# A fused attention and FFN layer on one core: the FFN's bias leaves TensorE and is added by the output transfers

## The chip, the cores and the metric

The kernel runs on one core of one Trainium2 chip. The metric is the device time of one execution in microseconds (us). Before the change it is 4342.03 us, the median of three runs (4333.88 to 4343.93).

## The reference, cut to what matters

```python
# x is (4, 2048, 512) float32, 16 heads of 32; the layer norms have no learned scale
x = x + attention(layernorm(x))          # softmax attention with a band bias, then Wo and bo
x = x + ffn(layernorm(x))                # x of this line is called x1 in the kernel

def ffn(x):                              # one linear layer
    xd = mx_quantize_and_scale_back(x)   # blocks of 32, scale = max|x| / 7.5, FP6 grid
    wd = mx_quantize_and_scale_back(weight)
    return xd @ wd.T + bias              # bias: 512 values, added to each of the 8192 rows
```

The output is therefore x1 + xd @ wd.T + bias for each of 8192 rows of 512 values, 16 MB in all.

## The kernel before, in words

The program has three stages, each a block of its own in which all engines start together.

`project` normalises x and makes q, k and v, which it leaves in device memory. `attend` runs over 64 units (16 groups of four heads in a batch, four chunks of 512 queries each), each unit over 16 steps `kt` of 128 keys. `finish` takes the 8192 rows in 16 chunks of 512 rows, and a chunk as four tiles of 128 rows.

**Attention.** TensorE makes the maxima of a unit ahead of its scores (L624), the scores (L643), the weighted sums (L657) and the sums of the softmax (L666). ScalarE makes the exponentials (L715), VectorE the maxima (L725) and the band (L752). GpSimd adds pairs of steps (L790) and issues five transfers a unit that add one pair buffer onto another in on-chip memory (L795, 1 MB each, `merged` counts them). The sync engine (SP) issues all other transfers in an order written out by hand: in each unit the stores of the unit before (L544, L548), the loads of q, k and v for the next group (L525, L530, L534), and at `kt` 14 the transfer L539, which puts the next unit's maxima into the row `shift` of its q tile. TensorE's first score of the next unit waits for it.

**The last stage.** For chunk c SP loads `o_raw` (L850), four transfers `o_rec` that spread each row of reciprocals over 32 partitions (L854) and `xb` (L859). GpSimd multiplies `o_raw` by `o_rec` (L901), ScalarE makes the high part (L930), GpSimd the low part (L905). TensorE projects (`out_project`, L1043), VectorE adds `xb` (x1, L980), takes the statistics, and after ScalarE's normalisation quantises (L952 to L965, the last gives `xd`). TensorE turns `xd` (`turn`, L1052), ScalarE and VectorE split it into `t_hi` and `t_lo` (L915, L972), TensorE multiplies by the FFN's weights (`linear`, L1070), and VectorE's `last_sum` (L996) adds x1 into `res`, one of two buffers, which SP stores (`store`, L863).

TensorE's order in iteration c is: `out_project(c + 1)` tiles 0 and 1, `turn(c)`, `out_project(c + 1)` tiles 2 and 3, `linear(c)`. Each tile of `out_project` or `linear` is 12 products of 128 x 128 by 128 x 512. In `linear` each tile begins with one more product, of a 2 x 128 tile of ones with `fb`, the bias in two parts (L1062). It starts the accumulation, so it puts the bias into the result. `fb` is prepared at the start of the stage by a load (L869), ScalarE (L935), VectorE (L1010) and a small transfer (L876).

SP's order in iteration c of this stage is `load_xb(c + 2)`, `load_o(c + 4)`, `store(c)`. `load_o(c)` waits until the low parts of chunk c - 2 are made. GpSimd's order is, for each chunk, four L901 and four L905. `last_sum` of chunk c waits until the store of chunk c - 2 has landed.

Of the kernel before, what the change touches and what calls it, by code (L numbers as in the profile page):

```python
# [14 lines left out]
P = 128  # L15
# [33 lines left out]
def f32(ap):  # L49

    return ap.bitcast(F32)


def build(nc, x, wq, wk, wv, wo, bq, bk, bv, bo, ocr_bias, ffn_w, ffn_b, out):
    x_ch = x.rearrange("(c t p) d -> c p t d", t=TT, p=P)
    out_ch = out.rearrange("(c t p) d -> c p t d", t=TT, p=P)

    def dram(name, shape):
        return nc.dram_tensor(name, shape, F32, kind="Internal").ap()


    q_hi_d, q_lo_d = dram("q_hi_d", (NHG * NCH, P, CH)), dram("q_lo_d", (NHG * NCH, P, CH))
    k_hi_d, k_lo_d = dram("k_hi_d", (NHG * NCH, P, CH)), dram("k_lo_d", (NHG * NCH, P, CH))
    v_d = dram("v_d", (NHG * NCH, TT, P, P))
    xb_d = dram("xb_d", (NCH, P, TT, D))
    wo_hi_d, wo_lo_d = dram("wo_hi_d", (P, KB, D)), dram("wo_lo_d", (P, KB, D))
    wd_hi_d, wd_lo_d = dram("wd_hi_d", (P, KB, D)), dram("wd_lo_d", (P, KB, D))
    o_d = dram("o_d", (NHG * NCH, P, CH))
    sum_d = dram("sum_d", (NHG * NCH, HG, CH))
    rec_d = dram("rec_d", (NHG * NCH, HG, CH))  # L70

    ctx = ExitStack()
    with ctx:
        def sem(name):
            return ctx.enter_context(nc.semaphore(name))

        ident = ctx.enter_context(nc.sbuf_tensor("ident", [P, P], F32))
        band_f = ctx.enter_context(nc.sbuf_tensor("band_f", [P, P + 2 * BAND_R], F32))
        project(nc, sem, ident, band_f, x_ch, wq, wk, wv, wo, bq, bk, bv, bo, ocr_bias, ffn_w,
                q_hi_d, q_lo_d, k_hi_d, k_lo_d, v_d, xb_d, wo_hi_d, wo_lo_d, wd_hi_d, wd_lo_d)  # L80
        attend(nc, sem, ident, band_f, q_hi_d, q_lo_d, k_hi_d, k_lo_d, v_d, o_d, sum_d, rec_d)
        finish(nc, sem, ident, ffn_b, xb_d, wo_hi_d, wo_lo_d, wd_hi_d, wd_lo_d, o_d, sum_d, rec_d, out_ch)
# [338 lines left out]
def attend(nc, sem, ident, band_f, q_hi_d, q_lo_d, k_hi_d, k_lo_d, v_d, o_d, sum_d, rec_d):  # L421
# [31 lines left out]
        sem("pv_done"), sem("sum_done"), sem("o_copied"), sem("sum_copied"), sem("o_out"), sem("sum_out"))  # L453
    den_loaded, den_inverted, rec_out = sem("den_loaded"), sem("den_inverted"), sem("rec_out")
# [46 lines left out]
    with ctx:  # L501
# [20 lines left out]
        def _(sp):  # L522
# [42 lines left out]
            for unit in range(NU + 1):  # L565
                g, u = unit // QC, unit % QC
                for kt in range(KT):
# [11 lines left out]
                    if unit == NU:  # L579
                        continue  # L580

# [20 lines left out]
            sp.wait_ge(sum_out, 16 * NU)  # L602
            sp.wait_ge(rec_out, 16 * (NG - 1))
# [195 lines left out]
def finish(nc, sem, ident, ffn_b, xb_d, wo_hi_d, wo_lo_d, wd_hi_d, wd_lo_d, o_d, sum_d, rec_d, out_ch):  # L799
# [5 lines left out]
    wo_in, wd_in, o_in, xb_in, fb_in = (  # L805
        [sem(f"wo_in{i}") for i in range(2)], sem("wd_in"), [sem(f"o_in{i}") for i in range(2)],
        [sem(f"xb_in{i}") for i in range(2)], sem("fb_in"))
# [3 lines left out]
    fb_split, fb_ready, consts2 = sem("fb_split"), sem("fb_ready"), sem("consts2")  # L811
# [9 lines left out]
    with ctx:  # L821
# [12 lines left out]
        fb_raw, fb_low = sb("fb_raw", [1, D]), sb("fb_low", [1, D], F32R)  # L834
        fb, ones2 = sb("fb", [2, D], F32R), sb("ones2", [2, P], F32R)
# [9 lines left out]
        def _(sp):  # L845
# [15 lines left out]
            def store(c):  # L861
                sp.wait_ge(res_ready, TT * c + TT)
                sp.dma_start(out_ch[c], res[:, c % 2]).then_inc(out_done[c % 2], 16)  # L863

# [4 lines left out]
            sp.dma_start(fb_raw[:], ffn_b.unsqueeze(0)).then_inc(fb_in, 16)  # L869
# [5 lines left out]
            sp.wait_ge(fb_split, 2)  # L875
            sp.dma_start(f32(fb[1:2, :]), f32(fb_low[:])).then_inc(fb_ready, 16)  # L876
# [4 lines left out]
            for c in range(NCH):  # L881
                if c + 2 < NCH:
                    load_xb(c + 2)
                if c + 4 < NCH:
                    load_o(c + 4)
                store(c)
# [4 lines left out]
        def _(pool):  # L891
            nc.gpsimd.memset(eps2[:], EPS).then_inc(consts2, 1)
            nc.gpsimd.memset(f32(ones2[:]), 1.0).then_inc(consts2, 1)
            for c in range(1, NCH):
                b = c % 2
# [7 lines left out]
                for g in range(NHG):  # L903
                    pool.wait_ge(o_high, NHG * c + g + 1)
                    nc.gpsimd.tensor_tensor(o_lo[:, b, g, :], o_raw[:, b, g, :], f32(o_hi[:, b, g, :]),  # L905
                                            ALU.subtract).then_inc(o_split, 1)

        @block.scalar
        def _(act):
# [23 lines left out]
            act.wait_ge(consts2, 2)  # L933
            act.wait_ge(fb_in, 16)
            nc.scalar.activation(fb[0:1, :], fb_raw[:], ACT.Copy).then_inc(fb_split, 1)  # L935
# [11 lines left out]
        def _(v):  # L947
# [61 lines left out]
            v.wait_ge(fb_split, 1)  # L1009
            nc.vector.tensor_tensor(fb_low[:], fb_raw[:], f32(fb[0:1, :]), ALU.subtract).then_inc(fb_split, 1)  # L1010
# [16 lines left out]
        def _(pe):  # L1027
# [27 lines left out]
            def linear(c):  # L1055
                for t in range(TT):
# [5 lines left out]
                    nc.tensor.matmul(ps_r[:, t, :], ones2[:], fb[:], start=True, stop=False)  # L1062
                    for k in range(KB):
# [5 lines left out]
                        for j, (lhs, rhs) in enumerate(terms):  # L1069
                            last = nc.tensor.matmul(ps_r[:, t, :], lhs, rhs, start=False,  # L1070
# [4 lines left out]
            for c in range(NCH):  # L1075
# [5 lines left out]
                if c == 0:  # L1081
                    pe.wait_ge(consts2, 2)
                    pe.wait_ge(fb_ready, 16)
# [28 lines left out]
```

## Time and profile before

| | |
|---|---|
| median of three runs | 4342.03 us (4333.88 to 4343.93) |
| the profiled execution | 4340.61 us, span of its instructions 4338.8 us |
| granted TensorE clock, mean | 0.983 of full speed |
| TensorE products busy | 4207.4 us, 97% of the span |
| VectorE, GpSimd, ScalarE busy | 3304.7, 2934.3, 2407.7 us |
| attention, about | 560 to 3860 us of the span |
| last stage, about | 3863 to 4339 us of the span |

A row of a window gives its start and end, its length, the busy time of TensorE's products, TensorE's weight loads, VectorE, ScalarE and GpSimd (with counts), the granted clock, the mean busy share of the 16 DMA engines and what they moved in GB/s. A row of a timeline gives the start, the length (of x4: of the four together), the engine, the line, the operation and its operands; in brackets stands how long the engine was idle before and what ended that. A TensorE product's own length overlaps the next one's, so the distance of two starts is what one costs. SPq is the issue of a transfer by SP.

### The profile page before, as it was taken

How to read it: one execution, taken by the hardware profiler on the slowest of the kernel's cores; microseconds unless marked ns; L12 is line 12 of the kernel's file. 1: busy time of each engine (PE TensorE's matmuls, PEld its weight loads, DVE VectorE, ACT ScalarE, POOL GpSimd, SP SyncE). 2: the span in 40 equal slices, each digit the busy share in tenths (PEclk: the TensorE clock that was granted, in tenths of full speed). 3: DMA queues.
4: the chain of work that ended last, by engine and by line, in shares of the span. 5: the costliest groups of instructions: out<-in, count | busy, mean ns of one | idle time of the engine just before them, and what ended most of it. 6: DMA issues, size and time to landing. Idle time of an engine off the chain costs nothing. (4 is left out here: it accounts for less than half of the span.)

```text
span 4338.8 us, 61851 instructions
## 1 busy us (share of the span) xinstructions
PE 4207.4 (97%) x22416; PEld 2580.4 (59%) x22416; DVE 3304.7 (76%) x5623; ACT 2407.7 (55%) x4652; POOL 2934.3 (68%) x983
## 2 busy tenths in 40 slices
PE   7999989999999999999999999999999999968999
PEld 6888855555555555555555555555555555526777
DVE  6444448888888888888888888888888888717776
ACT  2222216666666666666666666666666666623222
POOL 2111116888888887888888888888888888846552
PEclk9999979999999999999999999999999999979999
DMA  7666654676676766676766767666777666565442
GB/s 258 207 208 205 210 155 107 143 165 138 140 159 144 170 136 154 136 160 145 164 135 143 158 143 169 135 154 138 161 146 162 139 142 143 114 149 183 165 159 73
DMA packets 265423, 674.19 MB, mean 155 GB/s; under 512 B 26561, under 2 KB 93121, under 8 KB 219074
## 3 DMA queue, kind: packets, MB, share of 16 engines
q0 software_dynamic: 46080, 335.56, 38.7%
q1 hardware_dynamic: 219074, 335.10, 26.0%
q8 instruction: 161, 2.64, 0.2%
q14 instruction: 108, 0.88, 0.1%
HBM read 195.04 MB, written 139.46 MB: 77 GB/s over the span
## 5 line engine op out<-in xcount | busy, mean ns | idle before, releaser
L725 DVE TENSOR_REDUCE part_max<-ps_m 128x1 f32<-128x512 f32 x4096 | 2513.4, 680 | 501.3 <-PE ps_m L624 501.1
L790 POOL TENSOR_TENSOR pair<-p_sb 128x2048 f32<-128x2048 f32 x512 | 2413.8, 4723 | 419.0 <-ACT p_sb L715 211.7
L715 ACT ACTIVATE p_sb<-ps_s 128x512 f32<-128x512 f32 x4096 | 2084.5, 617 | 762.0 <-PE ps_s L643 758.3
L643 PE MATMUL ps_s<-q_st,k_st 97*128 97x512 f32 x4096 | 1687.5, 413 | 8.8 <-DMA q_st<-shift 6.3
L624 PE MATMUL ps_m<-k_st,q_st 96*128 96x512 f32 x4096 | 1641.8, 404 | 20.3 <-POOL k_st L779 20.1
L643 PEld LDWEIGHTS ps_s<-q_st,k_st 97*128 97x128 f32 x4096 | 772.7, 189 | 663.4 <-issue 430.4
L657 PE MATMUL ps_o<-p_sb,v_sb 128*32 128x512 f32 x8192 | 994.4, 603 | 13.3 <-DVE p_sb L752 5.6
L624 PEld LDWEIGHTS ps_m<-k_st,q_st 96*128 96x128 f32 x4096 | 786.8, 192 | 189.0 <-DVE part_max L725 37.2
L657 PEld LDWEIGHTS ps_o<-p_sb,v_sb 128*32 128x32 f32 x8192 | 225.0, 109 | 495.0 <-ACT p_sb L715 315.1
L795 POOL DMA_DIRECT2D pair<-pair x320 | 280.2, 876 | 182.1 <-POOL pair L790 153.7
L172 POOL TENSOR_TENSOR xb<-xin,bo_row 128x2048 f32<-128x2048 f32 x16 | 75.1, 4693 | 423.8 <-DMA xin<-in_x 413.3
L752 DVE TENSOR_TENSOR p_sb<-p_sb,band_f 128x520 f32<-128x520 f32 (+2 forms) x352 | 192.5, 575 | 51.3 <-ACT p_sb L715 51.3
L309 DVE SCALAR_TENSOR_TENSOR s_lo<-ps_p,bias,s_hi 128x512 fp32r<-128x512 f32 x128 | 96.0, 750 | 169.8 <-ACT s_hi L354 169.8
L354 ACT ACTIVATE s_hi<-ps_p,bias 128x512 fp32r<-128x512 f32 x128 | 88.1, 688 | 241.8 <-PE ps_p L405 233.4
L905 POOL TENSOR_TENSOR o_lo<-o_raw,o_hi 128x512 fp32r<-128x512 f32 x60 | 125.8, 2127 | 134.7 <-ACT o_hi L930 134.7
L405 PE MATMUL ps_p<-x_hi,w_hi 128*128 128x512 f32 x512 | 203.2, 397 | 4.2 <-DVE x_lo L294 4.1
L405 PE MATMUL ps_p<-x_hi,w_lo 128*128 128x512 f32 x512 | 200.8, 392 | 0.0
L405 PE MATMUL ps_p<-x_lo,w_hi 128*128 128x512 f32 x512 | 199.2, 389 | 0.0
L666 PE MATMUL ps_m<-pair,ones 128*32 128x512 f32 x1536 | 178.2, 595 | 9.1 <-DMA pair<-pair 9.1
L701 ACT ACTIVATE sum_st<-ps_m 128x512 f32<-128x512 f32 x64 | 38.2, 597 | 259.7 <-PE ps_m L666 259.7
L1043 PE MATMUL ps_r<-wo_hi,o_hi 128*128 128x512 f32 x256 | 103.6, 405 | 42.3 <-DVE o_lo L1005 27.3
L319 DVE TENSOR_TENSOR v_st<-ps_p,bv_row 128x512 f32<-128x512 f32 x64 | 44.1, 691 | 119.8 <-PE ps_p L405 119.8
(97 smaller groups left out, 2632.4 us busy)
## 6 DMA issues: line engine op xcount, KB each, us to landing
pair<-pair POOLq DMA_DIRECT2D x320, 1024.0 KB, 8.3
q_st<-q_hi_d SPq DMA_DIRECT2D x128, 256.0 KB, 6.9
k_st<-k_hi_d SPq DMA_DIRECT2D x128, 256.0 KB, 5.9
xin<-in_x SPq DMA_DIRECT2D x16, 1024.0 KB, 8.3
xb_d<-xb SPq DMA_DIRECT2D x16, 1024.0 KB, 5.2
q_hi_d<-s_hi SPq DMA_DIRECT2D x64, 256.0 KB, 2.0
q_lo_d<-s_lo SPq DMA_DIRECT2D x64, 256.0 KB, 2.3
k_hi_d<-s_hi SPq DMA_DIRECT2D x64, 256.0 KB, 2.3
```

Of the source, the lines that this page charges most:

```text
L405: last = nc.tensor.matmul(ps_p[:, n % RING], lhs, rhs, start=(k == 0 and j == 0), stop=(k == KB - 1 and j == 2))
L624: nc.tensor.matmul(ps_m[:, bank, :], q_st[0:ROWS, u, h, t * P:(t + 1) * P], k_st[0:ROWS, g % 2, n, h, :], start=True, stop=True).then_inc( ...
L643: nc.tensor.matmul(ps_s[:, (HG * s + h) % RING_S, :], k_st[0:ROWS + 1, unit // QC % 2, kt // TT, h, kt % TT * P:(kt % TT + 1) * P], q_st[0 ...
L657: last = nc.tensor.matmul(ps_o[h * HD:(h + 1) * HD, :], v_sb[:, kt, h * HD:(h + 1) * HD], p_sb[:, s % SLOTS, h, :], start=(kt == 0), stop= ...
L666: last = nc.tensor.matmul(ps_m[h * HD:(h + 1) * HD, bank, :], ones[:], pair[:, (PAIRS * unit + n) % PAIR_RING, h, :], start=(n == PAIRS - ...
L715: nc.scalar.activation(p_sb[:, s % SLOTS, h, :], ps_s[:, (HG * s + h) % RING_S, :], ACT.Exp, scale=SCALE).then_inc(p_ready, 1)
L725: nc.vector.tensor_reduce(part_max[:, unit % 2, col, n:n + 1], ps_m[:, max_place(unit, j) % RING_M, :], AX.X, ALU.max).then_inc(max_taken, 1)
L752: nc.vector.tensor_tensor(view, view, factor, ALU.mult).then_inc(banded, 1)
L790: nc.gpsimd.tensor_tensor(pair[:, m % PAIR_RING], p_sb[:, s % SLOTS], p_sb[:, (s + 1) % SLOTS], ALU.add).then_inc(paired, 1)
L795: pool.dma_start(pair[:, m % PAIR_RING], pair[:, (m - CHAINS) % PAIR_RING], accum_op=ALU.add).then_inc(merged[n % CHAINS], 16)
L905: nc.gpsimd.tensor_tensor(o_lo[:, b, g, :], o_raw[:, b, g, :], f32(o_hi[:, b, g, :]), ALU.subtract).then_inc(o_split, 1)
L1043: last = nc.tensor.matmul(ps_r[:, t, :], lhs, rhs, start=(k == 0 and j == 0), stop=(k == NHG - 1 and j == 2))
```

## The change

In attention SP gets one more transfer in each of the first 16 units, at `kt` 13: it fills one chunk of the output (1 MB, 512 rows of 2 KB) with the bias, read again and again from its 2 KB in device memory. A wait for all of them stands at the end of the stage. In the last stage the bias products, `fb` and all that prepared it are gone. The store moves from SP to GpSimd and becomes a transfer that adds `res` onto what stands in the output. GpSimd issues the store of chunk c - 4 ahead of its work on chunk c, and the last four stores behind all its other work.

```diff
 # attend, SP, in unit `unit` at step kt, ahead of put_shift(unit + 1) at kt 14
+                    if unit < NCH and kt == 13:
+                        sp.dma_start(out_ch[unit], ffn_b.unsqueeze(0).unsqueeze(0).to_broadcast([P, TT, D])).then_inc(bias_out, 16)
...
             sp.wait_ge(sum_out, 16 * NU)
+            sp.wait_ge(bias_out, 16 * NCH)
 # finish, SP
-            def store(c):
-                sp.wait_ge(res_ready, TT * c + TT)
-                sp.dma_start(out_ch[c], res[:, c % 2]).then_inc(out_done[c % 2], 16)
...
-            sp.dma_start(fb_raw[:], ffn_b.unsqueeze(0)).then_inc(fb_in, 16)
...
-            sp.wait_ge(fb_split, 2)
-            sp.dma_start(f32(fb[1:2, :]), f32(fb_low[:])).then_inc(fb_ready, 16)
...
                 if c + 4 < NCH:
                     load_o(c + 4)
-                store(c)
 # finish, GpSimd
-            nc.gpsimd.memset(f32(ones2[:]), 1.0).then_inc(consts2, 1)
+            def store(c):
+                pool.wait_ge(res_ready, TT * c + TT)
+                pool.dma_start(out_ch[c], res[:, c % 2], accum_op=ALU.add).then_inc(out_done[c % 2], 16)
+
             for c in range(1, NCH):
+                if c > 3:
+                    store(c - 4)
...
+            for c in range(NCH - 4, NCH):
+                store(c)
 # finish, ScalarE and VectorE
-            act.wait_ge(fb_in, 16)
-            nc.scalar.activation(fb[0:1, :], fb_raw[:], ACT.Copy).then_inc(fb_split, 1)
...
-            v.wait_ge(fb_split, 1)
-            nc.vector.tensor_tensor(fb_low[:], fb_raw[:], f32(fb[0:1, :]), ALU.subtract).then_inc(fb_split, 1)
 # finish, TensorE, linear(c), each of four tiles
-                    nc.tensor.matmul(ps_r[:, t, :], ones2[:], fb[:], start=True, stop=False)
...
-                            last = nc.tensor.matmul(ps_r[:, t, :], lhs, rhs, start=False,
+                            last = nc.tensor.matmul(ps_r[:, t, :], lhs, rhs, start=(k == 0 and j == 0),
```

## Rows read from the trace of the kernel before

**Rows 1.** Busy time by stretch: attention, and the last stage when steady
```profile
560.00:3860.00 3300.00, 3248.43 (x18147) 1819.15 (x18146) 2701.10 (x4609) 2156.23 (x4236) 2649.14 (x834) 0.99 0.68 146
4004.00:4200.00 196.00, 196.00 (x878) 151.48 (x876) 150.08 (x237) 53.76 (x95) 106.74 (x61) 1.00 0.47 167
```
**Rows 2.** The chain that ended last, shares of the span by line
```profile
by line: PE ps_r L1070 4.1%; PE ps_r L1043 3.5%; SPq L854 0.9%; PE ps_t L1052 0.6%; PE ps_r L1062 0.6%; DMA o_rec<-rec_d 0.3%; POOL o_raw L901 0.1%; SPq L866 0.1%; issue 0.1%; DVE res L996 0.1%; SPq L872 0.1%; DVE xd L965 0.1%; DVE y_q L960
```
**Rows 3.** Timeline of TensorE's products with and without a bias product between
```profile
4081.93 0.39 PE L1070 MATMUL ps_r<-wd_hi,t_lo 128*128 128x512 f32 x1
...
4082.16 0.39 PE L1043 MATMUL ps_r<-wo_hi,o_hi 128*128 128x512 f32 x1
...
4094.59 0.39 PE L1043 MATMUL ps_r<-wo_lo,o_hi 128*128 128x512 f32 x1
...
4094.91 0.50 PE L1062 MATMUL ps_r<-fb,ones 2*128 2x512 f32 x1
...
4095.33 0.50 PE L1070 MATMUL ps_r<-wd_hi,t_hi 128*128 128x512 f32 x1
...
4095.67 0.39 PE L1070 MATMUL ps_r<-wd_lo,t_hi 128*128 128x512 f32 x1
```
**Rows 4.** Timeline: xd made and turned, chunks 1 and 2, then steady
```profile
3953.92 2.28 DVE L965 TENSOR_TENSOR xd<-y_q,qs 128x2048 f32<-128x2048 fp8e4 x1
...
3956.87 1.91 PE L1052 MATMUL ps_t<-ident,xd 128*128 128x128 f32 x16
...
3977.99 3.44 DVE L965 TENSOR_TENSOR xd<-y_q,qs 128x2048 f32<-128x2048 fp8e4 x1
...
3983.01 1.91 PE L1052 MATMUL ps_t<-ident,xd 128*128 128x128 f32 x16
...
4081.20 2.28 DVE L965 TENSOR_TENSOR xd<-y_q,qs 128x2048 f32<-128x2048 fp8e4 x1
...
4087.60 1.91 PE L1052 MATMUL ps_t<-ident,xd 128*128 128x128 f32 x16
```
**Rows 5.** The end: the last turn and linear (timeline), the last sum (chain)
```profile
4317.92 1.97 PE L1052 MATMUL ps_t<-ident,xd 128*128 128x128 f32 x16 [0.28 <-DVE xd L965]
...
4320.24 0.50 PE L1070 MATMUL ps_r<-wd_hi,t_hi 128*128 128x512 f32 x1
...
4333.41 0.69 DVE res L996
```
**Rows 6.** Timeline of GpSimd, and VectorE's last sum of a chunk
```profile
4101.56 9.22 POOL L905 TENSOR_TENSOR o_lo<-o_raw,o_hi 128x512 fp32r<-128x512 f32 x4 [11.93 <-ACT o_hi L930]
...
4109.55 0.68 DVE L996 TENSOR_TENSOR res<-ps_r,x 128x512 f32<-128x512 f32 x1
...
4110.74 5.03 POOL L901 TENSOR_TENSOR o_raw<-o_raw,o_rec 128x512 f32<-128x512 f32 x4
```
**Rows 7.** Busy time by stretch: DMA idle, one merge alone, one chunk's transfers
```profile
928.00:936.00 8.00, 7.99 (x56) 4.05 (x55) 5.94 (x10) 4.04 (x9) 5.64 (x2) 1.00 0.00 0
946.00:952.00 6.00, 6.00 (x39) 3.38 (x35) 5.31 (x11) 4.06 (x8) 5.45 (x4) 1.00 0.87 176
4085.00:4094.00 9.00, 9.00 (x50) 7.68 (x49) 6.54 (x10) 2.07 (x4) 4.63 (x4) 1.00 0.99 342
4094.00:4104.80 10.80, 10.80 (x44) 7.54 (x42) 8.23 (x18) 5.32 (x9) 3.24 (x3) 1.00 0.27 104
```
**Rows 8.** The page: GpSimd's issue of an adding transfer, and its landing
```profile
L795 POOL DMA_DIRECT2D pair<-pair x320 | 280.2, 876 | 182.1 <-POOL pair L790 153.7
...
pair<-pair POOLq DMA_DIRECT2D x320, 1024.0 KB, 8.3
```
**Rows 9.** Timeline of SP in the fourth unit: last load, then the shift
```profile
841.37 0.38 SPq L534 DMA_DIRECT2D v_sb<-v_d  x1
855.10 0.52 SPq L539 DMA_DIRECT2D q_st<-shift  x1
```
**Rows 10.** Line L539 alone: who waited for it, us and times
```profile
  PEld ps_s L643: 13.7, 16
```

More of the change, by code:

```diff
@@ L80, in build @@
                 q_hi_d, q_lo_d, k_hi_d, k_lo_d, v_d, xb_d, wo_hi_d, wo_lo_d, wd_hi_d, wd_lo_d)
-        attend(nc, sem, ident, band_f, q_hi_d, q_lo_d, k_hi_d, k_lo_d, v_d, o_d, sum_d, rec_d)
-        finish(nc, sem, ident, ffn_b, xb_d, wo_hi_d, wo_lo_d, wd_hi_d, wd_lo_d, o_d, sum_d, rec_d, out_ch)
+        attend(nc, sem, ident, band_f, q_hi_d, q_lo_d, k_hi_d, k_lo_d, v_d, o_d, sum_d, rec_d, ffn_b, out_ch)
+        finish(nc, sem, ident, xb_d, wo_hi_d, wo_lo_d, wd_hi_d, wd_lo_d, o_d, sum_d, rec_d, out_ch)
 def blocks(ap):
@@ L418, in _, with attend @@
                     products(c, n)
-def attend(nc, sem, ident, band_f, q_hi_d, q_lo_d, k_hi_d, k_lo_d, v_d, o_d, sum_d, rec_d):
+def attend(nc, sem, ident, band_f, q_hi_d, q_lo_d, k_hi_d, k_lo_d, v_d, o_d, sum_d, rec_d, ffn_b, out_ch):
     NU = NG * QC
@@ L453, in attend @@
         sem("pv_done"), sem("sum_done"), sem("o_copied"), sem("sum_copied"), sem("o_out"), sem("sum_out"))
+    bias_out = sem("bias_out")
     den_loaded, den_inverted, rec_out = sem("den_loaded"), sem("den_inverted"), sem("rec_out")
@@ L796, in _, with finish @@
                                    accum_op=ALU.add).then_inc(merged[n % CHAINS], 16)
-def finish(nc, sem, ident, ffn_b, xb_d, wo_hi_d, wo_lo_d, wd_hi_d, wd_lo_d, o_d, sum_d, rec_d, out_ch):
-    wo_in, wd_in, o_in, xb_in, fb_in = (
+def finish(nc, sem, ident, xb_d, wo_hi_d, wo_lo_d, wd_hi_d, wd_lo_d, o_d, sum_d, rec_d, out_ch):
+    wo_in, wd_in, o_in, xb_in = (
         [sem(f"wo_in{i}") for i in range(2)], sem("wd_in"), [sem(f"o_in{i}") for i in range(2)],
-        [sem(f"xb_in{i}") for i in range(2)], sem("fb_in"))
+        [sem(f"xb_in{i}") for i in range(2)])
     rec_in = [sem(f"rec_in{i}") for i in range(2)]
@@ L810, in finish @@
     den_in, den_turned, rec_last = sem("den_in"), sem("den_turned"), sem("rec_last")
-    fb_split, fb_ready, consts2 = sem("fb_split"), sem("fb_ready"), sem("consts2")
+    consts2 = sem("consts2")
     out_projected, x1_ready, ln2_steps, std2_ready, rstd2_ready = (
@@ L932, in _ @@
             o_highs(0)
-            act.wait_ge(consts2, 2)
-            act.wait_ge(fb_in, 16)
-            nc.scalar.activation(fb[0:1, :], fb_raw[:], ACT.Copy).then_inc(fb_split, 1)
+            act.wait_ge(consts2, 1)
             o_highs(1)
@@ L1081, in _ @@
                 if c == 0:
-                    pe.wait_ge(consts2, 2)
-                    pe.wait_ge(fb_ready, 16)
                     pe.wait_ge(wd_in, 32)
```

2 lines of the change are left out of this document (removed).

## The prediction

> **What bounds the kernel now.** I read the page first, then the busy time by stretch. In attention TensorE's products are busy 3248 of 3300 us, and in the steady part of the last stage 196.00 of 196.00 us, at a granted clock of 1.00, the 2.4 GHz level [rows 1]. VectorE has about a quarter to spare there (150 of 196 us). The chain that ended last is, in the last stage, made of L1070, L1043, L1052 and L1062 [rows 2]: TensorE itself, with the bias products as 0.6% of the span, some 26 us, of their own. So what leaves TensorE's queue there is worth its full length, until another engine or a transfer becomes late. Then I read the timeline of one iteration of the last stage, its beginning and its end, and last the DMA engines' share, because the change moves work onto them.
>
> **What a bias product costs.** Two products with no bias between them start 0.23 us apart, also where the line changes from L1070 to L1043 and a wait on a semaphore already met stands between (4081.93 and 4082.16, the first two of [rows 3]). With a bias product between, the last product of L1043 starts at 4094.59, L1070's first at 4095.33 and its second at 4095.67 [rows 3]. That is 1.08 us where two steps of 0.23 would be 0.46. I count the whole difference, 0.62 us, and not the 0.42 us from the start of L1062 to the next, because the gaps on both sides go with the small 2-row product: they don't occur at the boundary in the first two rows. The first products behind it are a little slow too, and I round up to 0.65 us for each, 2.6 us for the four of a chunk. The period between two turns is 26.14 us (3956.87 to 3983.01) [rows 4]. It becomes 23.5 us if TensorE stays the bound.
>
> **Where the 16 iterations keep it and where not.** The turn of chunk c needs `xd`, the end of a chain on VectorE and ScalarE that starts when `out_project` ends. Between that start and the turn lie the four bias products, so the chain's slack shrinks by 2.6 us.
> - Steady: `xd` is ready at 4081.20 + 2.28 = 4083.48, the turn starts at 4087.60 [rows 4]. The slack is about 4.0 us (0.1 us of it taken by the last product), so 1.3 us are left. Iterations 2 to 13 keep all: 12 x 2.62 = 31.4 us.
> - Start: chunk 1 has 3956.87 - 3956.20 = 0.7 us and chunk 2 has 3983.01 - 3981.43 = 1.6 us [rows 4]. Both turns become bound by VectorE. Iterations 0 and 1 together give 0.65 + 1.55 = 2.2 us, not 4.6.
> - End: the turn of chunk 15 already waits for `xd` (0.28 us, "<-DVE xd") [rows 5], with nothing else for TensorE to do. Iteration 14 gives 0. In iteration 15 the first bias product hides mostly behind the split of the turned tile (L1070 starts at 4320.24, the turn ended at 4319.89), 0.3 us; the other three are on the path, 2.0 us. Together 2.3 us.
>
> The sum is 31.4 + 2.2 + 0 + 2.3 = 35.9 us saved.
>
> **The preparation of fb.** One load and one small transfer leave SP's queue, two operations of 0.6 us leave ScalarE and VectorE. They lie in the start of the stage, where the chain runs over SP's issues and the transfers `o_rec` [rows 2]. I take 0.5 us saved, between 0 and 1.1.
>
> **The store on GpSimd, steady.** GpSimd's low parts of a chunk end at 4110.74, when it goes on to L901; `res` of the right chunk is complete at 4109.55 + 0.68 = 4110.23 [rows 6]. Both move with the chain that starts at the end of `out_project`, so the new wait on `res_ready` costs at most about 0.5 us. The issue takes 0.88 us in attention [rows 8]. Behind it in GpSimd's queue stand the multiplications for the next chunk, and behind these it idles 11.93 us until ScalarE comes [rows 6]. With 2.6 us less period and 0.9 to 3.5 us of issue (3.5 if its length goes with the number of rows, four times as many as in a merge) 5.8 to 8.4 us of that are left. Cost: nothing; without the cover each iteration would pay the issue. `last_sum` of chunk c + 2 needs the store landed, more than a period after its issue, against 8.3 us to landing for a merge [rows 8]. The load of `xb` no longer waits behind the store in SP's queue and starts earlier.
>
> **The store's bytes.** This is the open cost. The transfers of one chunk keep the DMA engines busy from 4085 to 4104.8: all 16 for 9 us at 342 GB/s, then at a share of 0.27, four engines, for 10.8 us at 104 GB/s [rows 7]. The second part is `o_rec`. Those four engines are busy 19.8 us of 26.1. Three plain MB (`res`, `xb`, `o_raw`) take 3.15 us each of that. An adding transfer reads two operands: a merge of 1 MB takes 0.87 x 6 = 5.2 us of every engine, alone, at half the plain rate [rows 7]. Call the store's time A. The four engines then need 19.8 - 3.15 + A = 16.65 + A, and the period has 23.5: it holds up to A = 6.9. Between A = 5.2 (the merge, in pieces of 8 KB) and double that, 10.4 (if pieces of 2 KB in device memory suffer), I take 6, near the merge: plain 2 KB rows in device memory already move at 342 GB/s. Cost 0. The Trainium skill (Collectives: The Full Stack, "The bandwidth ceiling: the fold count and why AG ≠ RS ≠ AR") says that a reduce runs at half a copy's rate since the engine reads two sources, and that the add itself is free. By that rule A is twice 3.15, 6.3 us, and the sum is the same, with 0.6 us to spare. It is the rule that speaks against this change, and the merge's half rate agrees with it.
>
> **The end.** Now the last sum starts at 4333.41 and the span ends at 4338.8 [rows 5]: 0.7 us for the sum, 4.7 us for issue and landing of the store. An adding transfer takes 8.3 us in the median from issue to landing, beside other traffic [rows 8]. The last store has the engines to itself: between 6.9 us (4.7 plus the 2.2 us that the second operand adds to 3.15) and 13 us (A = 10.4 and 3.5 us of issue). I take 9.2, a cost of 4.5 us (2.2 to 8).
>
> **The fill in attention.** SP comes to the new transfer right behind its last load or store of the unit, long before `kt` 13 is computed: in the fourth unit at 841.8, while the shift follows at 855.10 [rows 9], 13.3 us later. The transfer takes 3.1 us of the engines at 342 GB/s; the slow end is 10 us, at the 104 GB/s with which `o_rec` reads a row of 2 KB again and again [rows 7]. There is room: the DMA engines are idle for 8 us at this place of a unit (from 928 on) [rows 7], and the five merges come after. The shift queues behind the fill only if the fill takes over 13 us. But the shift has no slack itself: TensorE waited for it in 16 of 64 units, 13.7 us in all [rows 10], so what it is late, TensorE pays. I take 1 us in all for 16 units (0 to 5). The wait at the end of the stage is met long before.
>
> **Sum.** -35.9 - 0.5 + 4.5 + 1 = -30.9 us. The profiled execution's 4340.6 us (span 4338.8 and 1.8 around it) becomes 4309.7. It lies 1.4 us under the median of the runs, so the median goes from 4342.0 to about 4311; I say 4310.
>
> **Rivals.**
> - *The four DMA engines become the bound.* Speaks for it: only 0.9 us of the period is free at A = 6. Against: the two-to-one rate of the merges. With A above 6.9 each of 12 iterations gives back A - 6.9, less some 8 us once for the idle time GpSimd has. A = 9: -30.9 + 25.2 - 8, so 4328. Chance 0.12.
> - *The same, far out: slower.* From A = 10.2 nothing is left, and at A = 12 it is -30.9 + 61.2 - 8 = +22, so 4364. It needs a store at more than twice a merge's price. Chance 0.07.
> - *The VectorE chain becomes the bound*, since 1.3 us are left: the store's issue or its traffic lengthens an operation of it. The `xd` of chunk 2 took 3.44 us where 2.28 is usual [rows 4]. One us too much costs 12 us: 4323. Chance 0.08.
> - *The fill makes the shift or the merges late*: x us in each of 16 units; 1 us gives 4326, 2 us take the whole gain, 4342, and 3 us end at 4358. Against: the idle DMA stretch. Chance 0.08, a quarter of it on the slow side.
> - *The gaps stay on TensorE*, and only the 0.42 us of the product itself goes: the 35.9 shrink by a third, 4322. Chance 0.05.
> - *The forecast as summed*, 4300 to 4320: chance 0.60.
>
> **How the numbers follow.** What a measurement of this kernel can tell from no change is about 0.3%, 13 us. The forecast, the gaps, most of the VectorE case and most of the first rival are faster by more than that: 0.60 + 0.05 + 0.07 + 0.07 = 0.79, and the milder half of the fill case makes it about 0.80, of which I give back 0.03 for what I have not seen: 0.77. Slower: 0.07 with a share of the fill case, 0.10. The rest, 0.13, is within 0.3%. The range goes from 4300 (all small costs at their low end, and 5 us of scatter as between the three runs) up to 4335, which takes in the first rival, the VectorE case and the gaps. The forecast's own range is 4300 to 4320.
>
> **What the new profile should show.** No L1062; products 0.23 us apart from `out_project` into `linear`; turns 23.5 us apart from chunk 3 on; `xd` ready 1.3 us ahead of a turn; PE busy for the whole steady stretch; GpSimd's store issued right behind the low parts, without a wait; the last sum at about 4298 and the end 9 us behind it; attention as long as before. Wrong would make it: an idle TensorE ahead of the turns, GpSimd waiting for `o_rec` in the steady part, TensorE waiting longer for the shift in the first 16 units, or a last store over 13 us.

## The result, and the profile after

The changed kernel takes 4320.21 us (median of 7 runs, 4316.0 to 4326.03) against 4339.31 us (7 runs, 4332.59 to 4343.93) of the kernel before, run beside it. The ratio is 0.9960, with a 95% interval of 0.9948 to 0.9971: 17 us less by the ratio (13 to 23), 19 us by the medians. Forecast were 31. The profiled execution took 4318.95 us with a span of 4317.1, so the two profiles differ by 21.7 us.

Busy time by stretch, in the columns of [rows 1]. First two windows that lie wholly in attention, 560 to 1440 us with the fills and 1470 to 3040 us without any, each before and then changed; then the changed kernel's last stage when steady, and two windows on its last iteration:

```profile
560.00:1440.00 880.00, 854.91 (x4613) 489.61 (x4613) 713.82 (x1219) 534.85 (x1047) 652.59 (x203) 0.96 0.67 144
560.00:1440.00 880.00, 852.73 (x4599) 487.20 (x4601) 710.71 (x1213) 531.15 (x1041) 646.60 (x201) 0.96 0.76 161
...
1470.00:3040.00 1570.00, 1560.12 (x8892) 878.11 (x8891) 1320.96 (x2265) 1059.69 (x2085) 1301.38 (x410) 1.00 0.70 149
1470.00:3040.00 1570.00, 1557.34 (x8865) 876.18 (x8863) 1318.49 (x2258) 1057.16 (x2081) 1296.49 (x410) 1.00 0.70 149
...
4011.00:4200.00 189.00, 189.00 (x904) 158.43 (x903) 161.94 (x260) 59.06 (x104) 126.04 (x74) 1.00 0.70 180
...
4290.00:4300.00 10.00, 8.84 (x40) 7.77 (x41) 5.17 (x7) 2.39 (x4) 1.28 (x1) 0.83 0.67 101
4291.00:4306.00 15.00, 14.56 (x64) 12.17 (x64) 5.79 (x10) 2.39 (x4) 1.28 (x1) 0.89 0.46 70
```

The steady part still belongs to TensorE: busy 189.00 of 189.00 us, granted 1.00, as in the second of [rows 1]. The DMA engines went from a share of 0.47 to 0.70 there without taking over. In attention TensorE's products are busy 2.2 us less than before in the stretch with the fills, with the DMA share up from 0.67 to 0.76, and 2.8 us less in the stretch behind it, where no fill is issued and the DMA share is as before. In the last iteration the granted clock is 0.83 and 0.89, which I had not foreseen.

The chain of the changed kernel, shares of the span by line, the answer to [rows 2], and two links of it (start, length, what):

```profile
by line: PE ps_r L1042 3.3%; PE ps_r L1068 3.0%; SPq L857 0.9%; PE ps_t L1051 0.6%; issue 0.6%; DMA o_rec<-rec_d 0.3%; DVE xd L966 0.2%; DVE peak L953 0.2%; DVE res L997 0.1%; POOL o_raw L902 0.1%; SPq L865 0.1%; DVE stats L983 0.1%; DVE x 
...
4083.67 5.46 PE ps_r L1042 x24
4089.13 10.88 PE ps_r L1068 x48
```

The bias products' 0.6% is gone, and `linear` of a chunk is 48 products in one piece. VectorE's `xd` went from 0.1% to 0.2%, because the turns of chunks 1 and 2 wait for it now. `issue` went from 0.1% to 0.6%, 26 us, but half of that is no loss: in the last iteration the chain follows GpSimd's queue through the 13.7 us that GpSimd waits for the last sum, and so leaves out the last turn and the last `linear`.

Timeline of the changed kernel, for [rows 3] to [rows 6]: start, length, engine, operation, and in brackets the idle time before:

```profile
3958.81 7.08 POOL L906 TENSOR_TENSOR o_lo<-o_raw,o_hi 128x512 fp32r<-128x512 f32 x4
3958.84 3.41 DVE L966 TENSOR_TENSOR xd<-y_q,qs 128x2048 f32<-128x2048 fp8e4 x1
...
3962.31 1.97 PE L1051 MATMUL ps_t<-ident,xd 128*128 128x128 f32 x16 [0.91 <-DVE xd L966]
...
3971.24 0.98 DVE L95 TENSOR_TENSOR mom<-stats 128x4 f32<-128x4 f32 x1
...
3972.22 1.26 DVE L97 TENSOR_TENSOR mom<-stats 128x4 f32<-128x4 f32 x1
...
3984.08 3.42 DVE L966 TENSOR_TENSOR xd<-y_q,qs 128x2048 f32<-128x2048 fp8e4 x1
...
3987.55 1.97 PE L1051 MATMUL ps_t<-ident,xd 128*128 128x128 f32 x16 [0.90 <-DVE xd L966]
...
4058.23 1.91 PE L1051 MATMUL ps_t<-ident,xd 128*128 128x128 f32 x16
...
4072.18 9.25 POOL L906 TENSOR_TENSOR o_lo<-o_raw,o_hi 128x512 fp32r<-128x512 f32 x4 [6.04 <-ACT o_hi L933]
...
4077.99 3.44 POOL L906 TENSOR_TENSOR o_lo<-o_raw,o_hi 128x512 fp32r<-128x512 f32 x1
4078.00 2.27 DVE L966 TENSOR_TENSOR xd<-y_q,qs 128x2048 f32<-128x2048 fp8e4 x1
...
4081.38 1.29 POOL L891 DMA_DIRECT2D out_y<-res  x1
...
4081.77 1.91 PE L1051 MATMUL ps_t<-ident,xd 128*128 128x128 f32 x16
4083.68 5.05 POOL L902 TENSOR_TENSOR o_raw<-o_raw,o_rec 128x512 f32<-128x512 f32 x4 [1.00 <-DMA o_rec<-rec_d]
...
4088.74 0.39 PE L1042 MATMUL ps_r<-wo_lo,o_hi 128*128 128x512 f32 x1
4088.97 0.39 PE L1068 MATMUL ps_r<-wd_hi,t_hi 128*128 128x512 f32 x1
...
4095.71 9.25 POOL L906 TENSOR_TENSOR o_lo<-o_raw,o_hi 128x512 fp32r<-128x512 f32 x4 [6.99 <-ACT o_hi L933]
...
4291.16 3.15 PE L1051 MATMUL ps_t<-ident,xd 128*128 128x128 f32 x16 [2.89 <-DVE xd L966]
...
4305.76 0.69 DVE L997 TENSOR_TENSOR res<-ps_r,x 128x512 f32<-128x512 f32 x1 [2.03 <-PE ps_r L1068]
...
4306.96 1.27 POOL L891 DMA_DIRECT2D out_y<-res  x1 [13.69 <-DVE res L997]
```

Read it from the middle. The last product of `out_project` and the first of `linear` start 0.23 us apart, so the gaps of [rows 3] went with the product. Two turns lie 23.54 us apart (4058.23 to 4081.77) where it was 26.14. `xd` is ready 1.5 us ahead of its turn (4078.00 + 2.27 against 4081.77). GpSimd issues the store in 1.29 us and then waits 1.00 us for `o_rec`. The turns of chunks 1 and 2 have 0.9 us of idle time before them, behind an `xd` of 3.4 us. The last turn comes after 2.89 us of idle TensorE and takes 3.15 us, where it had 0.28 and 1.97 [rows 5]. The last sum ends at 4306.45 and the span at 4317.1: 10.65 us, where [rows 5] have 4.7.

Cut at the turns, the two last stages compare like this (us; a stage starts at GpSimd's first operation in it; "the last sum" is the start of VectorE's last L997, 0.69 us before its end, here and in the stretches "from the last sum to the end" below):

| stretch | before | after | difference | forecast |
|---|---|---|---|---|
| start of the stage to turn of chunk 1 | 93.33 | 93.42 | +0.1 | } -2.2 -0.5 |
| turn 1 to turn 2 | 26.14 | 25.24 | -0.9 | } |
| turn 2 to turn 14 | 313.76 | 282.48 | -31.3 | -31.4 |
| turn 14 to turn 15 | 21.15 | 21.13 | 0.0 | 0 |
| turn 15 to the last sum | 15.49 | 14.60 | -0.9 | -2.3 |
| last sum to the end | 5.39 | 11.34 | +6.0 | +4.5 |
| the stage | 475.26 | 448.21 | -27.05 | -31.9 |
| ahead of the stage | 3863.54 | 3868.89 | +5.35 | +1 |

The steady gain came to 0.1 us as worked out. What is missing, 9 us by this pair of profiles and 12 by the medians, lies at the edges: in attention, in the last 15 us, and at the start of the stage.

### The profile page after: what moved, and what is told of

It reads as the page before. It is cut to its first block and busy times, and to the rows that moved or that the text cites. A ratio compares the mean times of both kernels' runs of the same rounds, so it can differ in the third digit from the quotient of the medians.

```text
span 4317.1 us, 61748 instructions
## 1 busy us (share of the span) xinstructions
PE 4168.2 (97%) x22352; PEld 2574.5 (60%) x22352; DVE 3308.0 (77%) x5622; ACT 2407.2 (56%) x4651; POOL 2949.7 (68%) x998
## 3 DMA queue, kind: packets, MB, share of 16 engines
q0 software_dynamic: 54528, 352.34, 41.2%
q1 hardware_dynamic: 219040, 335.09, 27.7%
## 5 line engine op out<-in xcount | busy, mean ns | idle before, releaser
L648 PE MATMUL ps_s<-q_st,k_st 97*128 97x512 f32 x4096 | 1687.3, 413 | 16.8 <-DMA q_st<-shift 14.7
L662 PE MATMUL ps_o<-p_sb,v_sb 128*32 128x512 f32 x8192 | 987.8, 599 | 14.3 <-DVE p_sb L757 7.3
L629 PEld LDWEIGHTS ps_m<-k_st,q_st 96*128 96x128 f32 x4096 | 786.8, 192 | 189.7 <-DVE part_max L730 38.3
```

What stands on the lines that cost most here:

```text
L629: nc.tensor.matmul(ps_m[:, bank, :], q_st[0:ROWS, u, h, t * P:(t + 1) * P], k_st[0:ROWS, g % 2, n, h, :], start=True, stop=True).then_inc( ...
L648: nc.tensor.matmul(ps_s[:, (HG * s + h) % RING_S, :], k_st[0:ROWS + 1, unit // QC % 2, kt // TT, h, kt % TT * P:(kt % TT + 1) * P], q_st[0 ...
L662: last = nc.tensor.matmul(ps_o[h * HD:(h + 1) * HD, :], v_sb[:, kt, h * HD:(h + 1) * HD], p_sb[:, s % SLOTS, h, :], start=(kt == 0), stop= ...
```

## The experiments

Ratios are to the kernel before, run beside each group of kernels on the same chip; a group is called a job. Jobs 1 to 4 had medians of it of 4339.51, 4340.18, 4340.83 and 4340.01 us.

**The change once more** (job 1, the same file).

> The changed kernel again, unaltered, on the chip of its neighbours. The first comparison gave a gain of 19 us where 31 were forecast, while the last stage of the profiled pair was 27 us shorter. If the missing part is scatter of the one profiled pair, the gain comes out here between 17 and 25 us, and the last stage is again 27 us shorter. Steady turns are 23.5 us apart.

Measured: 4319.31 us, ratio 0.9961 (0.9947 to 0.9976); its stage is 448.70 us. The cuts above repeat within 0.4 us each.

**Only the products gone** (job 1). No fill, a plain store from SP as before; the output lacks the bias.

```diff
-                    if unit < NCH and kt == 13:
-                        sp.dma_start(out_ch[unit], ffn_b...to_broadcast([P, TT, D])).then_inc(bias_out, 16)
...
 # finish: store(c) back in SP's loop behind load_o(c + 4)
+                sp.dma_start(out_ch[c], res[:, c % 2]).then_inc(out_done[c % 2], 16)
```

> Leaves out the bias altogether: no bias products, no preparation, no fill, and the plain store by the sync engine as before. Theory (products worth 0.65 us each, fill and tail cost the rest): steady turns 23.5 us apart, the end as before (5.4 us from the last sum), gain 31 to 36 us. Rival (the products are not worth that much over the runs, and the new stores and the fill cost nothing): the gain is that of the changed kernel, about 19 us.

Measured: 4303.12 us, ratio 0.9919 (0.9906 to 0.9933), 36.4 us less by the medians. The stage is 440.74 us, 34.5 less than before; the 1.9 us to the forecast's 36.4 are mostly iteration 15, which gave 0.95 here too. So the products and the preparation of `fb` are worth about what the sum said, and what is missing is the price of the bias's new way: 18 us by the two ratios of this job.

**Only the fill, in the kernel before** (e2, job 1), **and a fill in each of the 64 units** (e4, job 1).

```diff
 # e2, in the kernel before
+                    if unit < NCH and kt == 13:
+                        sp.dma_start(out_ch[unit], ffn_b...to_broadcast([P, TT, D])).then_inc(bias_out, 16)
 # e4
+                    if kt == 13:
+                        at_least(sp, bias_out, 16 * unit)
+                        sp.dma_start(out_ch[unit % NCH], ffn_b...to_broadcast([P, TT, D])).then_inc(bias_out, 16)
```

> The kernel before, with only the fill of the output with the bias added in attention (the last stage stores over it, so the fill is work for nothing). Theory (the fill costs little, the missing 12 us lie in the end of the program and its start): 0 to 3 us slower than before. Rival (the fill makes the shift late and is the main loss): 5 to 10 us slower, with more waits of TensorE for the shift in the first 16 units.

> As the one before, but with a fill in each of the 64 units (each part of the output is filled four times, work for nothing): four times the suspected cost. If a fill costs x in a unit, the kernel is 64x slower than before: 3 to 10 us if the fill costs little (0.05 to 0.15 us a unit), 20 to 40 us if it is the main loss (0.3 to 0.6 us a unit).

Measured: e2 4344.15 us, ratio 1.0013 (1.0004 to 1.0022); e4 4354.19 us, ratio 1.0034 (1.0021 to 1.0048). That is 4.6 us for 16 fills (2 to 10 by the interval) and 14.7 us for 64, or 0.23 us a fill, 3.7 for 16. Both lie between the small cost and the main loss that were expected. The last stages of both are as before (475.00 and 474.30 us).

The profiles give a second measure, the time at which the last stage starts. It is 3859.8 to 3863.5 us in the four kernels that fill nothing (before, e1, and e8 and e10 below), and 3865.4 to 3876.2 us in the six that fill 15 or 16 chunks from the one row (the changed kernel twice, e2, e3, e6, e9); the means are 3861.8 and 3869.8. By this the fill costs 8 us. The highest of them is e2, whose profiled execution, at 4353.35 us, was its slowest. So the price is some 4 to 8 us.

Where it is paid, the tile `shift` alone from 640 to 1440 us tells, all but the last of the 16 shifts that follow a fill: first before, then the changed kernel, then e2, who waited for it (us, times) and the time from issue to landing:

```profile
  PEld ps_s L643: 3.4, 3
  PE ps_s L643: 2.0, 3
...
DMA to landing us min/median/max: 1.8/3.0/5.7
```

```profile
  PEld ps_s L648: 8.3, 8
  PE ps_s L648: 4.8, 7
...
DMA to landing us min/median/max: 1.9/4.6/5.8
```

```profile
  PEld ps_s L647: 8.4, 9
  PE ps_s L647: 4.7, 6
...
DMA to landing us min/median/max: 1.9/4.7/6.2
```

The shift takes 1.6 us longer to land in the median, and TensorE's products wait for it 7 times instead of 3. The fill itself is mostly gone by then: in the changed kernel it is issued 13.3 to 18.9 us ahead of the shift (41 in the first unit), and 14 of the 16 land after 10.3 to 11.7 us. What is under way when the shift is issued are GpSimd's merges, the transfers that add one pair buffer onto another, which the fill has pushed back. In the fourth unit the merge that is issued 0.6 us after the fill lands after 15.4 us, where the same one before took 7.0, the next after 14.3 instead of 9.1, and the shift after 5.6 instead of 2.6. All merges from 640 to 1440 us, KB each and median us from issue to landing, before and in the changed kernel:

```profile
pair<-pair POOLq DMA_DIRECT2D x76, 1024.0 KB, 8.3
```

```profile
pair<-pair POOLq DMA_DIRECT2D x75, 1024.0 KB, 10.9
```

So it is the fourth rival's mechanism ("the shift or the merges late", x us in each of 16 units), with x = 0.23 to 0.5. In e4 the same tile cost TensorE's products, over all 64 units, 21.9 us of waits (38.3 for the weight loads) where before has 6.3 and 13.7 (the latter is [rows 10]): 15.6 us more, beside 14.7 us of time.

Part of the price falls where nothing is filled. From 1470 us on, the products' waits for the shift are 4.3 us before, 5.2 in e1, 5.7 in e8 and 6.5 in e10, which fill nothing, but 9.0 in the changed kernel (8.3 the second time), 7.6 in e2 and 7.6 to 9.8 in all others with 15 or 16 fills. Why the later units lose too was not settled.

The queue that SP feeds, on the pages of before and of e4 (packets, MB, share of 16 engines), gives the fill's own size:

```profile
q1 hardware_dynamic: 219074, 335.10, 26.0%
```

```profile
q1 hardware_dynamic: 252866, 402.21, 35.4%
```

64 fills of 1 MB (67.11 MB in the page's millions of bytes) took (0.354 x 4357.1 - 0.260 x 4338.8) / 64 = 6.5 us of every engine each, with the spans of the two executions. The fill was sized at 3.1, with 10 as the slow end.

**The store on GpSimd without the add** (e3, job 2). The fill stays; the output then lacks the bias.

```diff
-                pool.dma_start(out_ch[c], res[:, c % 2], accum_op=ALU.add)
+                pool.dma_start(out_ch[c], res[:, c % 2])
```

> The changed kernel with its stores still issued by GpSimd, but plain, without the add (the output lacks the bias; the fill stays and is overwritten). The changed kernel's last sum to end is 11.3 us, the kernel before's 5.4. Theory (the add is the price: a second operand, read in device memory): 6 to 7.5 us from the last sum to the end, gain some 24 us. Rival (GpSimd's issue is the price): it stays at 10 to 11 us, and the gain at 20. The turns of chunks 1 and 2, 25.3 us apart in the changed kernel and 23.6 where no store was GpSimd's, tell the same of the early part: 23.6 if the add did it, 25.3 if GpSimd's issue or its place in the order did.

Measured: 4317.26 us, ratio 0.9944 (0.9931 to 0.9957). Timeline of its end, the last sum and the last store:

```profile
4309.10 0.69 DVE L997 TENSOR_TENSOR res<-ps_r,x 128x512 f32<-128x512 f32 x1 [2.03 <-PE ps_r L1068]
...
4310.09 0.75 POOL L891 DMA_DIRECT2D out_y<-res  x1 [13.96 <-DVE res L997]
```

Its span is 4315.6 us, so from the last sum to the end it is 6.50 us, where e1 has 5.33 and the changed kernel 11.34. GpSimd in SP's place costs 1.2 us of the tail; the add costs 4.8. The issue takes 0.75 us without the add and 1.29 with it. Turns 1 and 2 are 25.22 us apart, as with the add (25.24), and 23.62 in e1: the 1.6 us lost there come with the store's move from SP to GpSimd and not from the adding.

The last store has the DMA engines to itself, so its own size can be read. Busy time by stretch from its issue to the end, before and in the changed kernel:

```profile
4334.10:4338.80 4.70, 0.00 (x0) 0.00 (x0) 0.01 (x1) 0.00 (x0) 0.00 (x0) 0.99 0.60 223
```

```profile
4307.00:4317.10 10.10, 0.00 (x0) 0.00 (x0) 0.00 (x0) 0.00 (x0) 1.24 (x1) 0.59 0.70 104
```

A plain store takes 4.70 x 0.60 = 2.8 us of every engine, the adding one 10.1 x 0.70 = 7.1, which is 2.5 times as much. These 4.3 us and 0.5 us more of issue are the 4.8.

**The fill copied from the chunk before** (e5, job 2). Only the first chunk reads the 2 KB row; each later one reads the 512 rows that the last fill wrote.

```diff
+                        at_least(sp, bias_out, 16 * unit)
+                        src = out_ch[unit - 1] if unit else ffn_b...to_broadcast([P, TT, D])
-                        sp.dma_start(out_ch[unit], ffn_b...to_broadcast([P, TT, D])).then_inc(bias_out, 16)
+                        sp.dma_start(out_ch[unit], src).then_inc(bias_out, 16)
```

> The changed kernel, but each fill after the first copies the part of the output filled one unit earlier, instead of reading the 2 KB of the bias 512 times. Theory (the fill takes some 7.4 us of every DMA engine because all of them read one row, and that time makes the shift late): the fill lands in 5 to 7 us instead of 10.8, TensorE waits for the shift in the first 16 units as before the change (2 to 3 us in all), the kernel is 2 to 4 us faster than the changed one. Rival (any 1 MB from device memory to device memory costs that): landing 10 to 11 us, the same time as the changed kernel, a gain of 20 us.

Measured: 4312.32 us, ratio 0.9946 (0.9934 to 0.9959). Its transfers by kind (KB each, median us from issue to landing):

```profile
out_y<-out_y SPq DMA_DIRECT2D x15, 1024.0 KB, 6.6
out_y<-in_ffn_b SPq DMA_DIRECT2D x1, 1024.0 KB, 10.4
```

Its tile `shift` in the first 16 units, as above:

```profile
  PEld ps_s L650: 5.4, 6
  PE ps_s L650: 2.7, 5
...
DMA to landing us min/median/max: 1.8/3.6/5.7
```

A fill lands after 6.6 us instead of 10.4 although it writes the same bytes. By the shares of SP's queue, 27.7% of 4317.1 us and 26.7% of 4309.2, a copied fill takes 3 us of every engine less than one from the row. The shift's landing is back to 3.6, and the products' waits in these units are 2.7 us, nearly those of before (2.0). So in these units most of the price was that of reading one small row 512 times. Behind them it is not mended: from 1470 us on the waits are 7.6 us, and the last stage of the three kernels with copies (e5, e7, e11) starts at 3861.2 to 3871.5 us, 3866.6 in the mean, between those without fills and those that read the row. By the time alone the gain over the changed kernel, 7 us by the medians of two jobs or 6 by the ratios, is inside the intervals, so that copying shortens the kernel is likely and not shown.

**The last chunk without the add** (e6, job 2) **and both** (e7, job 2). GpSimd adds the bias's row to x1 of chunk 15 while TensorE is busy, and SP stores that chunk tile by tile, plain. 15 fills are left.

```diff
+                sp.wait_ge(res_ready, TT * (NCH - 1) + t + 1)
+                sp.dma_start(out_ch[NCH - 1][:, t], res[:, (NCH - 1) % 2, t]).then_inc(tail_out, 16)
...
+                nc.gpsimd.tensor_tensor(x1b[:, t, :], x1[:, (NCH - 1) % 2, t, :], fb_row2[:], ALU.add).then_inc(x1b_ready, 1)
```

> The changed kernel with another way for the last of 16 chunks only: GpSimd, idle there, adds a row of the bias to x1 ahead of the last sum, and the sync engine stores the sum plainly, tile by tile. If the adding store's landing is what stands behind the last sum, the 11.3 us become 3.5 to 5, and the gain over before grows from 20 to about 26 us. If GpSimd's additions slow VectorE's chain to the last turn (it shares nothing with it in the kernel before), the stretch from the turn of chunk 14 to that of chunk 15, 21.1 us, grows by 1 to 3 us and eats part of it.

> The two before together: the fills copy, and the last chunk is stored plainly. If both costs are separate, their gains add: 28 to 30 us faster than the kernel before, 8 to 10 faster than the changed one.

Measured: e6 4315.16 us, ratio 0.9945 (0.9932 to 0.9957); e7 4309.87 us, ratio 0.9940 (0.9921 to 0.9960; one of its 12 runs, at 4360.61 us, widens this interval). From the last sum to the end it is 3.16 and 3.24 us where the changed kernel has 11.34. The stages are 441.74 and 441.20 us. The tail was a price of its own and can be had back whole, and 2 us more than before with it. The additions lengthen the stretch from turn 14 to turn 15 only from 21.13 to 21.60 us, where 1 to 3 us were feared. By the times e6 and e7 can't be told from each other, nor either from the changed kernel if the ratios of two jobs are compared; the gain of e6 is read from its stage.

**The bias on GpSimd for every chunk** (e8, job 3). No fill, no adding transfer; stores from SP, plain.

```diff
+            def add_row(c):
+                at_least(pool, res_ready, TT * c)
+                for t in range(TT):
...
+                    nc.gpsimd.tensor_tensor(x1b[:, t, :], x1[:, c % 2, t, :], fb_row2[:], ALU.add).then_inc(x1b_ready, 1)
```

> Another way to add the bias: no fill, no adding store, no bias products. In the last stage GpSimd, idle for 8 to 12 us of an iteration, adds a row of the bias to x1 in a buffer of its own (four operations of 1.25 us a chunk), the last sum reads that buffer, and the sync engine stores plainly (the last chunk tile by tile). With the products gone alone the gain was 36 us. Theory (GpSimd's work fits into its idle time): steady turns 23.5 us apart, 3 us from the last sum to the end, gain 33 to 38 us. Rival (its additions lengthen VectorE's operations beside them, of whose chain only 1.3 us of slack are left): turns 24 to 25.5 us apart and a gain of 10 to 30 us.

Measured: 4317.59 us, ratio 0.9947 (0.9933 to 0.9961). Attention and the tail (3.23 us) were mended, but turns 1 and 2 are 27.79 us apart (23.62 in e1) and turns 2 to 14 take 287.74 us (282.40). Timeline of e8 at a place where it loses:

```profile
4044.39 7.09 POOL L921 TENSOR_TENSOR o_lo<-o_raw,o_hi 128x512 fp32r<-128x512 f32 x4 [4.87 <-ACT o_hi L948]
...
4050.22 3.42 DVE L981 TENSOR_TENSOR xd<-y_q,qs 128x2048 f32<-128x2048 fp8e4 x1
...
4051.45 7.08 POOL L915 TENSOR_TENSOR o_raw<-o_raw,o_rec 128x512 f32<-128x512 f32 x4
...
4053.69 1.97 PE L1067 MATMUL ps_t<-ident,xd 128*128 128x128 f32 x16 [0.93 <-DVE xd L981]
```

`xd` starts inside GpSimd's low parts, takes 3.42 us instead of 2.28, and the turn waits. Of the steady periods every third is 25.1 to 25.2 us long and the others are 23.5 to 23.6. In these iterations GpSimd's operations and VectorE's lie on each other. So it went as the rival said: taking the work off the DMA engines moved the loss to VectorE's chain.

**TensorE kept at work ahead of the last turn** (e9, job 3), **and with e8** (e10, job 3).

```diff
             def turn(c):
+                at_least(pe, t_lo_done, KB * c)
+                if c == NCH - 1:
+                    for i in range(24):
+                        nc.tensor.transpose(ps_t[:, i % KB, 0:P], ident[:], ident[:])
                 pe.wait_ge(xd_ready, c + 1)
-                at_least(pe, t_lo_done, KB * c)
```

> The changed kernel with 24 transposes of the identity (work for nothing, 2.6 us) in TensorE's idle time ahead of the last turn. From that turn to the last sum the changed kernel and all others without bias products took 14.5 us, the kernel before 15.5, where I had counted 13.2: in the profile the granted clock falls to 0.83 in that stretch, after 2.9 us in which TensorE idles. Theory (the idle time brings the lower clock, and that eats the gain): 13.0 to 13.4 us, 1.2 us less in all. Rival (the products are slower there for another reason): 14.5 us again.

> The bias on GpSimd and the transposes for nothing together. If both hold, it is the fastest of all: 34 to 39 us faster than the kernel before. If GpSimd's additions slow VectorE's chain, the turns show it as in the kernel without the transposes.

Measured: e9 4321.73 us, ratio 0.9957 (0.9943 to 0.9971); e10 4317.17 us, ratio 0.9944 (0.9931 to 0.9958). Timeline of e9:

```profile
4289.10 2.78 PE L1050 MATMUL ps_t<-ident 128*128 128x128 f32 x24
4292.14 1.97 PE L1054 MATMUL ps_t<-ident,xd 128*128 128x128 f32 x16 [0.26 <-DVE xd L966]
```

Busy time by stretch of e9, from its last turn on:

```profile
4292.00:4306.00 14.00, 13.10 (x64) 10.66 (x64) 5.77 (x10) 2.07 (x4) 1.28 (x1) 1.00 0.51 75
```

The granted clock is 1.00 instead of 0.89, the turn takes 1.97 us instead of 3.15, and from the last turn to the last sum it is 13.33 us instead of 14.60. 1.27 us is too little to see in the time. In e10 the loss of e8 stays: turns 2 to 14 take 289.33 us, the stage 449.59, and the 34 to 39 us did not come.

**All that mended something** (e11, job 4): e7 with e9's transposes.

> The changed kernel with the three mends that each showed its effect in a trace: fills by copy, the last chunk stored plainly tile by tile, transposes for nothing ahead of the last turn. If they add, the last stage is 35 us shorter than before and the whole 30 to 33 us faster than the kernel before, 10 to 12 faster than the changed one. If the fill by copy gave nothing beyond scatter, 26 to 29.

Measured: 4310.83 us, ratio 0.9932 (0.9919 to 0.9946), 29 us less than before; the stage is 440.52 us, 0.2 us under e1's, which leaves the bias out altogether. It has the lowest ratio of the kernels that compute all of the reference. Against the changed kernel's 0.9960 (0.9948 to 0.9971, another job) the intervals do not overlap, if barely; from e7 (0.9921 to 0.9960) it can't be told.

## Why the prediction was right or wrong, point by point

**The products: right.** Twelve periods gave 31.3 us where 31.4 were worked out, and e1 alone took 34.5 us off the stage where -35.9 and -0.5 stand. That it took just 36.4 off the time is partly luck, since 1.9 us of that lie outside the changed stage. Counting the whole difference of the boundary, the gaps with it, was the right reading of [rows 3]. The rival that the gaps stay is out.

**The store's bytes: right in the steady part.** A was taken as 6. By the pages' shares of the queue that GpSimd feeds, 41.2% of 4317.1 us against 38.7% of 4338.8, the 16 stores took (1778.6 - 1679.1) / 16 = 6.2 us of every engine each. The four engines had 0.7 us to spare, and the turns stay 23.54 us apart, so both of the first rivals are out. The Trainium skill (Collectives: The Full Stack, "The bandwidth ceiling: the fold count and why AG ≠ RS ≠ AR") gives a reduce half a copy's rate. By the 3.15 us that were taken for a plain MB that is an estimate of 6.3 us, near the 6.2; but a plain store alone takes 2.8 us and the adding one 7.1, so for this store the measurement says 2.5 to 1. The 3.15 stands in no row: 1.05 million bytes at the 342 GB/s of [rows 7] take 3.07 us.

**GpSimd: nearly right.** The issue took 1.29 us (0.9 to 3.5 were allowed) and costs nothing when steady. Said was that GpSimd would not wait for `o_rec` there. It does, 1.00 us in the iteration shown and 0 to 2.2 in the later ones, and the idle time ahead of the low parts that follow, 6.99 us at 4095.71, covers it.

**The start: mis-sized, nothing is left of it.** Turns 1 and 2 were to give 2.2 us, and less preparation of `fb` 0.5. This pair gave 0.8, the second run of the changed kernel 0.2. From the start of the stage to turn 2 it is 118.5 to 119.5 us in the three kernels with bias products and 118.7 to 120.0 in the eight with the store on GpSimd; to turn 1 it is 92.4 to 93.3 us with the preparation and 93.4 to 95.0 without, so no run shows the 0.5 either. In e1, with the store on SP, turn 2 comes after 117.3 us. The step took VectorE's chain as it was. The chain depends on where GpSimd's operations fall: with the store on GpSimd, issued ahead of its work on chunk 4 while VectorE is at chunk 2 (after and e3), `xd` of chunk 2 takes 3.4 us, and two of the 0.16 us operations on the moments take 0.98 and 1.26 (0.88 and 1.32). In e1 `xd` of that chunk takes 2.28, and the period there is 23.62. The store did not bring the collision in, since before `xd` of chunk 2 took 3.44 too [rows 4]; it kept it where e1 is rid of it. The VectorE rival named this operation and mistook the place: it costs 1.6 us once, not 12 times.

**The fill: the mechanism was a rival's, the size was wrong.** The term of +1 us measured 4 to 8 (e2: 4.6, e4: 3.7 for 16, the profiles: 8), around the upper bound of 5. The step failed where it said "There is room" and weighed only whether the shift queues behind the fill. The fill takes 6.5 us of every engine and not 3.1, and it pushes back the merges, whose median landing went from 8.3 to 10.9 us and which the shift then meets: its own landing went from 3.0 to 4.6 us. The idle stretch of [rows 7] was also misplaced. It ends at 937 us, and SP comes to that unit's fill only behind the store of the sums and the loads of k, at 941.11 in the changed kernel, with the first merge 7 us behind it.

**The end: mis-sized.** 9.2 us were said from the last sum's end to the span's and 10.65 came, a cost of 6.0 instead of 4.5, inside the bounds of 2.2 to 8. e3 shows that 4.8 of it are the add. The estimate lay between a plain store's 4.7 with 2.2 for the second operand, and 13. The last adding store ends 10.1 us after its issue (4306.96 to 4317.1), later than a merge beside other traffic (8.3), so doubling the engines' share of a plain store was the wrong model for its length: the add brought 4.3 us of every engine and not the 2.2 of its low end.

**Iteration 15: mis-sized.** 2.3 us were said and 0.9 came. Nothing was said of the clock. With the bias products gone, TensorE was idle for 2.89 us ahead of the last turn where it had been for 0.28; in the window from that turn on the granted clock is 0.89 and the turn itself took 3.15 us. e9 gives the 1.27 us back, and then it is 2.2.

**The sum again.** The time, 4320.2 us, lies in the range of 4300 to 4335 and just beyond the upper end of the forecast's own, 4320. The terms at the edges all missed to the same side. The stage gave 27.05 us, and the fill took 4.6 to 8: 19 to 22 us, against 19 by the medians. One thing stays open. In job 1 e1 and the changed kernel differ by 18 us (9 to 27 if the two ratios are taken as independent), while the parts (6.0 for the tail, 1.6 for turn 2, 4.6 for the fill) make 12.2, or 15.6 with 8 for the fill. The rest is inside the intervals, and the start of the last stage varies by 4 us among the four kernels whose attention is the same, so I don't give it a cause. The median of before was also 1 to 3 us lower in these runs than in the first three, which has no part in the ratio.

## What to carry to other kernels

Work that leaves a saturated engine can be priced by the distance of its neighbours' starts with and without it, and here that price held to a tenth of a microsecond; what it costs elsewhere was paid at the edges, in the first and last iterations and in the stage that takes in the new transfers, so price these one by one. A transfer in a stage with "free" DMA engines can still delay a small transfer that an engine waits for, even when it lands before that is issued, by pushing back the large ones between: here 1.6 us in the median. Look at what is queued between the two, and price a new transfer by a profile of a like one, not by its bytes. At the end of this kernel nothing hid the store: let the last one be plain, small and issued tile by tile, whatever the others are.

## What the runs showed of the hardware

- 1 MB filled by reading one row of 2 KB 512 times took 6.5 us of every DMA engine and 10.8 us to land; copied from 512 different rows it took 3 us of every engine less and landed in 6.6 us. The written side was the same.
- An adding store of 512 rows of 2 KB into device memory took 6.2 us of every engine in the mean and 7.1 alone at the very end, where a plain one took 2.8. There it was 10.65 us from the sum that feeds it to the end of the span, where a plain one took 4.7 from SP and 5.8 from GpSimd. GpSimd's issue took 1.29 us with the add, 0.75 without.
- 2.89 us of idle TensorE were followed by a granted clock of 0.89 over the next 15 us, so part of them at the 1.2 GHz level and the rest at 2.4; with transposes in that gap it was 1.00. The turn at the start of that stretch took 3.15 us in place of 1.97.
- VectorE's `xd` took 3.4 instead of 2.28 us, and operations of 0.16 us took up to 1.32, in stretches in which GpSimd worked on operands of its own; one of GpSimd's multiplications takes 5.04 / 4 = 1.26 us. The Trainium skill (SBUF — State Buffer, "Terms", "shared port pair") says that the two engines share a pair of ports which one holds for a whole instruction while the other waits, and the length of one GpSimd operation agrees with that. In the steady iterations `xd` keeps its 2.28 us, and there GpSimd pays: its low part beside `xd` (4077.99) takes 3.44 us instead of 1.26, longer by 2.18, about the length of `xd`. Which of the two is held when both start within 0.05 us was not settled.
